# Moving x statistics, Gram products, expert choices and row sends to other places of a hand-written order

## The chip, the cores and the metric

One NeuronCore of a Trainium2 chip runs the whole program. The metric is the device time of one execution in microseconds. The matmul engine is TensorE (PE in the rows, PEld its weight loads), the others are VectorE (DVE), ScalarE (ACT), GpSimd (POOL) and SyncE (SP, which only issues DMAs here).

## What is computed

Two layers over x of shape 4 x 2048 x 256, in float32: an attention over channels, then a mixture of experts.

```python
x = x + layernorm(attn(layernorm(x)))          # attn: per head, softmax over DH x DH products qk . qk
h = layernorm(x) * g + b
logits = h @ Wr;  top 2 of 7 experts, gates = softmax of the two logits
pos = running count of tokens per expert       # a token above the capacity is dropped
routed = sum over choices of gate * (silu(h_e @ W1) * (h_e @ W3)) @ W2
shared = silu(h @ W1s) * (h @ W3s) @ W2s
x = x + layernorm(routed + shared)
```

## The kernel before

A **chunk** is 512 rows; a batch has four of them, q = 0 to 3. The attention of a batch needs only the Gram product of its normalised x (256 x 256, over all 2048 rows); from it comes one matrix M per batch, and the attention's output is x times M. So every batch b has these **steps**, each a few instructions on one or more engines:

- x steps, per chunk: `x_first` (SP loads x chunks 0 and 1), `x_stats` (DVE mean and variance, POOL the power -1/2), `x_norm` (DVE normalises into one of two buffers; behind it SP loads the chunk after next), `x_high` and `x_part` (ACT and DVE split the normalised x into two halves for exact products), `x_gram` (PE, 8 matmuls of 512 columns into banks 4 and 5).
- turned x, per chunk: `x_turned` (SP loads the transposed raw x, 512 KB, into the same two buffers `xin` that held x), `x_keep` (ACT copies its high half), `x_low` (DVE the rest).
- M: the steps `m_gram` to `m_low`, small and in a chain across PE, ACT and DVE.
- output, per chunk: `o_mix` (PE, x times M), `o_stats`, `o_norm`, `o_apply`, `o_add`, `u_stats`, `u_norm`, `u_turn0`, `u_turn1`, `u_route`, `u_copy`: second layernorm, transposition, logits.
- routing, per pair of chunks: `r_top` and `r_next` (DVE, the best and second expert), `u_count` (PE, running counts by matmul), `u_slot` (DVE, adds the carry), `u_place` (DVE, the target rows), then `u_send0` to `u_send3` per chunk (POOL, two indirect DMAs each) that write the rows to memory by expert.

Under all this runs the **shared expert** over the first 13 chunks. Each chunk has eight m-steps; PE does the up products of one m (12 matmuls of 512 columns, a product for the silu first and then one for the factor), then the down products of m-3 (12 matmuls of 256 columns). ACT does the silu (L1114), DVE multiplies (L1801), ACT makes the high half (`high`, L1066) and DVE the low half (`low`, L1777), one m behind. Only two banks take the up products of these chunks, so the up products of m wait for the silu and the multiplication of m-1.

All steps hang on **places**: place 16n+2m lies behind the up products of m-step m of chunk n, place 16n+2m+1 behind the down products that follow. An order written by hand, `schedule`, holds for each place the steps that come there, and every engine walks through the same list (`attend`, L546), doing those that it has a part in. So a step's place sets the order on five in-order queues at once. Within a place, steps of the earlier batch come first. On ACT place 2m comes after the silu of m and place 2m+1 after `high` of m-1; on DVE place 2m comes after the multiplication of m and 2m+1 after `low` of m-1 (and, for m = 6, after the split of the next chunk's h, L1771). ACT also takes the finished chunk before out of its banks (`take_y`) at m = 2, after `high` of m-1.

Waits that matter: `x_gram` waits for `x_part` of its chunk. The load of turned chunk 0 waits for `x_norm` of chunk 2, that of turned chunk 1 for `x_norm` of chunk 3, since they take the buffers that these read:

```python
            def load_turned(b, q):
                ...
                if b > 0 and q > 1:
                    sp.wait_ge(xtlo_ok, b * GB + (q - 1))
                    sp.sem_inc(sp_go, 1)
                sp.wait_ge(xn_ok, OPEN + b * GB + (q % 2 + 3))
                sp.sem_inc(sp_go, 1)
                sp.dma_start(turned_at(b, q).rearrange("p k n -> p (k n)"), x_turned[b * GB + q]).then_inc(xT_in[q], 16)
```

`u_count` waits for `r_next`; `u_turn0` of chunk 3 waits for `u_norm` of that chunk and for `u_slot` of the first pair. After the 13 chunks come the seven routed experts and three held chunks of the shared expert (from about 610 us); their code is the same before and after.

Of the kernel before, what the change touches and what calls it, by code (L numbers as in the profile page):

```python
# [45 lines left out]
def sandwich_kernel(nc, x_in, Wqk, Wv, Wo, tau, ln_g, ln_b, Wr, W1, W3, W2, W1s, W3s, W2s, x_turned, out):  # L46
# [51 lines left out]
    with ExitStack() as ctx:  # L98
# [366 lines left out]
        def put(b, origin, q, names):  # L465
            for name, at in names:
                schedule[BEFORE + origin + at].append((name, b, q))

        X_STEPS = (("x_stats", 0), ("x_norm", 3), ("x_high", 4), ("x_part", 5))
        GRAM_AT = (None, (9, 12, 16, 19), (7, 11, 15, 19), (7, 11, 15, 19))  # L470
        T_STEPS = (("x_turned", (13, 16, 18, 20)), ("x_keep", (16, 18, 22, 25)), ("x_low", (17, 19, 24, 28)))
        M_STEPS = ("m_gram", "m_turn", "m_cross", "m_sym", "m_times_wqk", "m_keep_t", "m_dots", "m_pick", "m_rowdiag",
                   "m_logits", "m_exp", "m_softmax", "m_times_wo", "m_keep_n", "m_times_wv", "m_high", "m_low")
# [11 lines left out]
        def put_routing(b, origin, pairs, firsts, apart):  # L485
            for pair in range(2):
                put(b, origin, pair, zip(R_NAMES, pairs[pair]))
            for q in range(GB):
                put(b, origin, q, [(f"u_send{t}", firsts[q] + apart * t) for t in range(GT)])
# [23 lines left out]

        X_AT, M_AT, MIX_AT = (None, 14, 66, 115), (None, 34, 87, 136), (None, 46, 101, 148)
        for b in range(1, B):
            put(b, X_AT[b] - 8 if b > 1 else 0, 0, [("x_first", 0)])
            for q in range(GB):
                put(b, X_AT[b] + 4 * q, q, X_STEPS)
                put(b, X_AT[b], q, [(name, places[q] - (b == 1 and q == 3 and name == "x_low")) for name, places in T_STEPS])
                put(b, X_AT[b], q, [("x_gram", GRAM_AT[b][q])])  # L520
            put(b, M_AT[b], 0, zip(M_STEPS, M_AT_PLACES[b]))
            for q in range(GB):
                put(b, MIX_AT[b] + 5 * q, q, O_STEPS)
            if b == 1:
                put_routing(b, MIX_AT[b], ((21, 21, 23, 24, 25), (32, 34, 38, 39, 40)), (27, 35, 43, 51), 2)
            elif b == 2:
                put_routing(b, MIX_AT[b], ((21, 21, 22, 23, 24), (31, 32, 33, 34, 35)), (26, 33, 40, 47), 2)
            else:
                put_routing(b, MIX_AT[b], ((21, 21, 24, 25, 26), (31, 31, 34, 34, 35)), (27, 31, 36, 40), 1)
        for j in range(PIECES):  # L530
# [1456 lines left out]
```

## Time and profile before

| | |
|---|---|
| time, median of 3 runs (lowest, highest) | 1077.16 us (1076.68, 1078.14) |
| the profiled execution: its time, its span | 1078.76 us, 1077.0 us |
| granted TensorE clock, mean over the span | 0.995 |
| PE busy, DVE busy | 1046.2 us, 658.9 us |

The span is counted from the first to the last instruction; the profile gives every instruction its start, and for each idle time the engine that ended it. The places 0 to 207 lie between 54 us and 610 us, so a place is 2.7 us on average. PE's rows tell at which place it is: 12 products with `sb_h`, then an even place, 12 with `sb_act`, then an odd one. `L1210` rows are the Gram products, `L1345` rows the start of a count.

### The profile page before, as it was taken

To read this page: it belongs to the slowest core of one execution; us is meant where nothing else is said; L and a number is where in the kernel's file an instruction comes from. 1 tells how busy PE (TensorE), PEld (TensorE's weight loads), DVE (VectorE), ACT (ScalarE), POOL (GpSimd) and SP (SyncE) were. 2 spreads that over 40 slices of the span, in tenths; PEclk is the share of its full clock that TensorE was granted. 3 is DMA by queue.
4 is the path that set the end of the run, shared out by engine and by line. 5 is a ranking of instruction groups with operands and counts; after the bars stand their busy time and mean duration, and the time that the engine had idled before them with its cause. 6 is when DMAs were issued, how large, how long until landed. Compare 5 with 4: busy or idle time off the path is not lost.

```text
span 1077.0 us, 19528 instructions
## 1 busy us (share of the span) xinstructions
PE 1046.2 (97%) x6863; PEld 956.7 (89%) x6863; DVE 658.9 (61%) x1717; ACT 504.3 (47%) x895; POOL 385.4 (36%) x348
## 2 busy tenths in 40 slices
PE   7999999999999989999999999999999999999997
PEld 6888888887889877888888999999999999998886
DVE  7768863787655797537755345455454546364785
ACT  4344452443443444434444345545464636354773
POOL 3011441513531116421167313344443333123563
PEclk9999999999999999999999999999999999999999
DMA  8332351434522135423244145243433423256695
GB/s 285 110 101 83 125 186 40 142 118 142 183 74 89 60 138 165 159 81 136 108 141 162 38 168 145 53 125 71 110 91 86 118 55 86 45 159 228 113 205 114
DMA packets 47949, 130.20 MB, mean 121 GB/s; under 512 B 10356, under 2 KB 18168, under 8 KB 47872
## 3 DMA queue, kind: packets, MB, share of 16 engines
q1 hardware_dynamic: 29376, 93.87, 25.7%
q0 software_dynamic: 18496, 35.35, 14.5%
q8 instruction: 43, 0.70, 0.3%
q14 instruction: 34, 0.28, 0.1%
HBM read 74.24 MB, written 54.93 MB: 120 GB/s over the span
## 4 chain that ended last, share of the span: by engine, by line
PE 88%; DVE 8%; issue 2%; ACT 1%; DMA 1%; DVEq 0%; SPq 0%; POOL 0%; ACTq 0%
PE bank L1191 27%; PE bank L1193 26%; PE bank L1192 26%; PE bank L1210 3%; DVE sb_act L1801 1%; PE bank L1317 1%; PE bank L1370 1%; ACT sb_ln_o L999 1%; PE bank L1270 1%; DVE sb_st L1494 1%; PE bank L1329 1%; DVE sb_act_lo L1777 1%; DMA sb_ysb<-in_L_ffn_W2s_dram 1%; PE bank L1240 1%; DVE sb_stX L1494 0%
## 5 line engine op out<-in xcount | busy, mean ns | idle before, releaser
L1801 DVE TENSOR_TENSOR sb_act<-bank,sb_act 128x512 f32<-128x512 f32 (+2 forms) x240 | 148.6, 619 | 344.0 <-PE bank L1193 319.6
L1191 PE MATMUL bank<-sb_h_hi,sb_wup_lo 128*128 128x512 f32 (+2 forms) x960 | 354.3, 369 | 2.3 <-ACT sb_act L1114 1.5
L1193 PE MATMUL bank<-sb_h_hi,sb_wup_hi 128*128 128x512 f32 (+2 forms) x960 | 349.8, 364 | 0.0
L1192 PE MATMUL bank<-sb_h_lo,sb_wup_hi 128*128 128x512 f32 (+2 forms) x960 | 349.5, 364 | 0.0
L1114 ACT ACTIVATE sb_act<-bank 128x512 f32<-128x512 f32 (+2 forms) x240 | 129.9, 541 | 356.2 <-PE bank L1193 346.0
L1191 PE MATMUL bank<-sb_wdn_hi,sb_act_lo 128*128 128x256 f32 (+1 forms) x848 | 244.8, 289 | 0.6 <-DVE sb_act_lo L1777 0.6
L1193 PE MATMUL bank<-sb_wdn_hi,sb_act_hi 128*128 128x256 f32 (+1 forms) x848 | 238.9, 282 | 0.0
L1192 PE MATMUL bank<-sb_wdn_lo,sb_act_hi 128*128 128x256 f32 (+1 forms) x848 | 238.8, 282 | 0.0
L1191 PEld LDWEIGHTS bank<-sb_h_hi,sb_wup_lo 128*128 128x128 f32 x960 | 180.7, 188 | 23.2 <-DVE sb_act L1801 2.1
L1193 PEld LDWEIGHTS bank<-sb_h_hi,sb_wup_hi 128*128 128x128 f32 x960 | 180.6, 188 | 22.6
L1192 PEld LDWEIGHTS bank<-sb_h_lo,sb_wup_hi 128*128 128x128 f32 x960 | 181.1, 189 | 17.0
L1777 DVE TENSOR_TENSOR sb_act_lo<-sb_act,sb_act_hi 128x512 fp32r<-128x512 f32 (+2 forms) x240 | 147.4, 614 | 27.3 <-ACT sb_act_hi L1066 25.7
L1191 PEld LDWEIGHTS bank<-sb_wdn_hi,sb_act_lo 128*128 128x128 f32 (+1 forms) x848 | 158.3, 187 | 5.7 <-issue 1.2
L1192 PEld LDWEIGHTS bank<-sb_wdn_lo,sb_act_hi 128*128 128x128 f32 (+1 forms) x848 | 158.3, 187 | 3.4
L1193 PEld LDWEIGHTS bank<-sb_wdn_hi,sb_act_hi 128*128 128x128 f32 (+1 forms) x848 | 158.2, 187 | 0.0
L1066 ACT ACTIVATE sb_act_hi<-sb_act 128x512 fp32r<-128x512 f32 (+2 forms) x240 | 136.6, 569 | 1.1 <-DVE sb_act L1801 1.1
L892 POOL DMA_INDIRECT y_scratch<-sb_ysb,sb_scur x42 | 77.3, 1840 | 155.2 <-ACT sb_ysb L1103 90.4
L804 POOL TENSOR_TENSOR sb_rstdB<-sb_veB,sb_mhalf 128x4 f32<-128x4 f32 x16 | 19.1, 1193 | 174.1 <-DVE sb_veB L1620 174.1
L820 POOL DMA_INDIRECT sent_scratch<-sb_rows,sb_sendto x64 | 68.5, 1070 | 30.5 <-issue 18.8
L853 POOL DMA_INDIRECT sb_rows<-sent_scratch,sb_gcur x42 | 43.7, 1041 | 76.9 <-issue 52.2
L999 ACT ACTIVATE sb_ln_o<-bank,sb_nbiasB,sb_rstdB 128x256 f32<-128x256 f32 x64 | 30.9, 563 | 34.9 <-DVE sb_nbiasB L1625 34.9
L800 POOL TENSOR_TENSOR sb_rstdX<-sb_veX,sb_mhalf 128x4 f32<-128x4 f32 x16 | 20.1, 1254 | 72.7 <-DVE sb_veX L1512 72.7
(268 smaller groups left out, 1239.4 us busy)
## 6 DMA issues: line engine op xcount, KB each, us to landing
sb_xin<-in_L_ffn_W_dram SPq DMA_DIRECT2D x28, 512.0 KB, 3.6
sb_x<-in_L_attn_x_dram SPq DMA_DIRECT2D x16, 512.0 KB, 4.2
out_dram<-sb_x SPq DMA_DIRECT2D x16, 512.0 KB, 3.5
sb_xin<-in_L_attn_x_dram SPq DMA_DIRECT2D x14, 512.0 KB, 4.6
sb_xin<-in_x_turned_dram SPq DMA_DIRECT2D x14, 512.0 KB, 4.5
sb_xn<-in_L_ffn_W_dram SPq DMA_DIRECT2D x14, 512.0 KB
hT_scratch<-sb_hr SPq DMA_DIRECT2D x13, 512.0 KB, 2.9
sb_hfull<-hT_scratch SPq DMA_DIRECT2D x13, 512.0 KB, 4.2
```

Of the source, the lines that this page charges most:

```text
L820: pool.indirect_dma_start(sent_d, bass.IndirectOffsetOnAxis(ap=sendto[:, q, t, c:c + 1], axis=0), u[q][:, t, :], None).then_inc(sent[q], 16)
L853: pool.indirect_dma_start(rows[0:w, part, t, :], None, sent_d, bass.IndirectOffsetOnAxis(ap=gcur[0:w, part, t:t + 1], axis=0)).then_inc(ga ...
L892: pool.indirect_dma_start(y_d, bass.IndirectOffsetOnAxis(ap=scur[0:w, par, part, t:t + 1], axis=0), ysb[0:w, part, t, :], None, compute_op ...
L999: ins = s.activation(ln_o[:, t, :], bank[o_bank(b, q) + t // 2][:, (t % 2) * D:(t % 2 + 1) * D], ACT.Identity, scale=rstdB[:, t:t + 1], bi ...
L1066: s.activation(act_hi[:, m % 4, 0:c.w], act[:, m % 3, 0:c.w], ACT.Copy).then_inc(ahi_ok, 1)
L1114: s.activation(act[:, m % 3, 0:c.w], a[:, 0:c.w], ACT.Silu).then_inc(silu_ok, 1)
L1191: t_.matmul(o, a_lo, b_hi, start=start, stop=False, skip_group_check=True)
L1192: t_.matmul(o, a_hi, b_lo, start=False, stop=False, skip_group_check=True)
L1193: return t_.matmul(o, a_hi, b_hi, start=False, stop=stop, skip_group_check=True)
L1210: ins = t_.matmul(bank[4 + k][:, o:c], a[:, k * P:(k + 1) * P], a[:, o:c], start=(q == 0 and t == 0), stop=(q == GB - 1 and t == GT - 1))
L1777: v.tensor_tensor(act_lo[:, m % 4, 0:c.w], act[:, m % 3, 0:c.w], act_hi[:, m % 4, 0:c.w].bitcast(F32), ALU.subtract).then_inc(alo_ok, 1)
L1801: v.tensor_tensor(act[:, m % 3, 0:c.w], bank[(4 if c.wide and m % 2 else 0) + 1][:, 0:c.w], act[:, m % 3, 0:c.w], ALU.mult).then_inc(act_o ...
```

## The change

No instruction is added or taken away. For batches 2 and 3 the x steps get a table of their own, `X_PLACES`, in place of one pattern; the table of batch 1 gives its old places. The turned-x steps, the M steps and the output steps stay where they are. In the routing of batches 1 and 2 some places move.

| step | before (chunks 0, 1, 2, 3) | after |
|---|---|---|
| batch 2: `x_first` | 58 | 56 |
| `x_stats` | 66, 70, 74, 78 | 64, 72, 76, 80 |
| `x_norm` | 69, 73, 77, 81 | 69, 75, 79, 83 |
| `x_high` | 70, 74, 78, 82 | 70, 76, 80, 84 |
| `x_part` | 71, 75, 79, 83 | 71, 77, 81, 85 |
| `x_gram` | 73, 77, 81, 85 | 75, 79, 83, 86 |
| batch 3: `x_first` | 107 | 101 |
| `x_stats` | 115, 119, 123, 127 | 109, 114, 124, 128 |
| `x_norm` | 118, 122, 126, 130 | 115, 124, 128, 132 |
| `x_high` | 119, 123, 127, 131 | 116, 125, 129, 133 |
| `x_part` | 120, 124, 128, 132 | 117, 126, 130, 134 |
| `x_gram` | 122, 126, 130, 134 | 122, 128, 132, 135 |
| not moved: `x_turned`, `x_keep`, `x_low` of chunks 0, 1 | batch 2: 79, 82; 82, 84; 83, 85. Batch 3: 128, 131; 131, 133; 132, 134 | the same |
| batch 1 routing, pairs 0 and 1: `r_next`, `u_count`, `u_slot`, `u_place` | 67, 69, 70, 71; 80, 84, 85, 86 | 67, 69, 70, 74; 78, 82, 83, 89 |
| batch 1, first send of each chunk | 73, 81, 89, 97 | 76, 83, 91, 98 |
| batch 2 routing | 122, 123, 124, 125; 133, 134, 135, 136 | 122, 124, 125, 127; 132, 135, 136, 140 |
| batch 2, first send of each chunk | 127, 134, 141, 148 | 129, 136, 143, 150 |

```diff
@@ -466,8 +466,11 @@
             for name, at in names:
                 schedule[BEFORE + origin + at].append((name, b, q))
 
-        X_STEPS = (("x_stats", 0), ("x_norm", 3), ("x_high", 4), ("x_part", 5))
-        GRAM_AT = (None, (9, 12, 16, 19), (7, 11, 15, 19), (7, 11, 15, 19))
+        X_NAMES = ("x_stats", "x_norm", "x_high", "x_part", "x_gram")
+        X_PLACES = (None, ((14, 17, 18, 19, 23), (18, 21, 22, 23, 26), (22, 25, 26, 27, 30), (26, 29, 30, 31, 33)),
+                    ((64, 69, 70, 71, 75), (72, 75, 76, 77, 79), (76, 79, 80, 81, 83), (80, 83, 84, 85, 86)),
+                    ((109, 115, 116, 117, 122), (114, 124, 125, 126, 128), (124, 128, 129, 130, 132),
+                     (128, 132, 133, 134, 135)))
         T_STEPS = (("x_turned", (13, 16, 18, 20)), ("x_keep", (16, 18, 22, 25)), ("x_low", (17, 19, 24, 28)))
         M_STEPS = ("m_gram", "m_turn", "m_cross", "m_sym", "m_times_wqk", "m_keep_t", "m_dots", "m_pick", "m_rowdiag",
                    "m_logits", "m_exp", "m_softmax", "m_times_wo", "m_keep_n", "m_times_wv", "m_high", "m_low")
@@ -513,18 +516,17 @@
 
         X_AT, M_AT, MIX_AT = (None, 14, 66, 115), (None, 34, 87, 136), (None, 46, 101, 148)
         for b in range(1, B):
-            put(b, X_AT[b] - 8 if b > 1 else 0, 0, [("x_first", 0)])
+            put(b, (0, 0, 56, 101)[b], 0, [("x_first", 0)])
             for q in range(GB):
-                put(b, X_AT[b] + 4 * q, q, X_STEPS)
+                put(b, 0, q, zip(X_NAMES, X_PLACES[b][q]))
                 put(b, X_AT[b], q, [(name, places[q] - (b == 1 and q == 3 and name == "x_low")) for name, places in T_STEPS])
-                put(b, X_AT[b], q, [("x_gram", GRAM_AT[b][q])])
             put(b, M_AT[b], 0, zip(M_STEPS, M_AT_PLACES[b]))
             for q in range(GB):
                 put(b, MIX_AT[b] + 5 * q, q, O_STEPS)
             if b == 1:
-                put_routing(b, MIX_AT[b], ((21, 21, 23, 24, 25), (32, 34, 38, 39, 40)), (27, 35, 43, 51), 2)
+                put_routing(b, MIX_AT[b], ((21, 21, 23, 24, 28), (32, 32, 36, 37, 43)), (30, 37, 45, 52), 2)
             elif b == 2:
-                put_routing(b, MIX_AT[b], ((21, 21, 22, 23, 24), (31, 32, 33, 34, 35)), (26, 33, 40, 47), 2)
+                put_routing(b, MIX_AT[b], ((21, 21, 23, 24, 26), (31, 31, 34, 35, 39)), (28, 35, 42, 49), 2)
             else:
                 put_routing(b, MIX_AT[b], ((21, 21, 24, 25, 26), (31, 31, 34, 34, 35)), (27, 31, 36, 40), 1)
         for j in range(PIECES):
```

## Rows read from the trace of the kernel before

**Rows 1.** The page, part 1: busy us (share of span) x instructions.

```profile
PE 1046.2 (97%) x6863; PEld 956.7 (89%) x6863; DVE 658.9 (61%) x1717; ACT 504.3 (47%) x895; POOL 385.4 (36%) x348
```

**Rows 2.** Timeline of PE, places 69 to 87: start, length, [idle before <-releaser].

```profile
236.12 0.37 PE L1345 MATMUL bank<-sb_oh,sb_earlier 128*128 128x112 bf16 x4 [1.42 <-DVE sb_oh L1701]
...
249.23 2.61 PE L1210 MATMUL bank<-sb_wdn_hi 128*128 128x512 f32 x8 [2.24 <-DVE sb_wdn_hi L1631]
...
257.39 0.50 PE L1191 MATMUL bank<-sb_h_hi,sb_wup_lo 128*128 128x512 f32 x1
...
260.29 0.28 PE L1191 MATMUL bank<-sb_wdn_hi,sb_act_lo 128*128 128x256 f32 x1
...
261.72 1.80 PE L1210 MATMUL bank<-sb_wdn_lo 128*128 128x512 f32 x8
...
263.36 0.39 PE L1191 MATMUL bank<-sb_h_hi,sb_wup_lo 128*128 128x512 f32 x1
...
283.10 1.79 PE L1210 MATMUL bank<-sb_wdn_lo 128*128 128x512 f32 x8
```

**Rows 3.** Timeline of PE, places 121 to 135.

```profile
384.99 0.50 PE L1191 MATMUL bank<-sb_h_hi,sb_wup_lo 128*128 128x512 f32 x1 [1.46 <-ACT sb_act L1114]
...
393.36 0.37 PE L1345 MATMUL bank<-sb_oh,sb_earlier 128*128 128x112 bf16 x4 [1.39 <-DVE sb_oh L1701]
...
426.72 0.37 PE L1345 MATMUL bank<-sb_oh,sb_earlier 128*128 128x112 bf16 x4 [2.01 <-DVE sb_oh L1701]
...
427.26 3.01 PE L1210 MATMUL bank<-sb_wdn_lo 128*128 128x512 f32 x8
```

**Rows 4.** Windows after two of the waits: busy of each engine, PEclk, DMA share, GB/s.

```profile
249.20:256.00 6.80, 6.77 (x26) 5.77 (x27) 2.98 (x7) 1.89 (x3) 1.84 (x2) 0.75 0.50 164
426.70:433.50 6.80, 6.78 (x42) 6.19 (x43) 2.80 (x7) 0.00 (x0) 4.29 (x4) 0.75 0.72 236
```

**Rows 5.** Timeline of DVE: what it idled for at places 64, 109 and 114.

```profile
226.81 0.69 DVE L1777 TENSOR_TENSOR sb_act_lo<-sb_act,sb_act_hi 128x512 fp32r<-128x512 f32 x1 [2.52 <-ACT sb_act_hi L1066]
...
353.67 0.69 DVE L1801 TENSOR_TENSOR sb_act<-bank,sb_act 128x512 f32<-128x512 f32 x1 [2.48 <-ACT sb_act L1114]
...
367.84 0.69 DVE L1777 TENSOR_TENSOR sb_act_lo<-sb_act,sb_act_hi 128x512 fp32r<-128x512 f32 x1 [2.52 <-ACT sb_act_hi L1066]
```

**Rows 6.** Timeline of DVE: one of each kind of work, and what follows it.

```profile
230.71 1.40 DVE L1494 BATCH_NORM_STATS2 sb_stX<-sb_xin 128x6 f32<-128x256 f32 x4
...
232.75 0.69 DVE L1777 TENSOR_TENSOR sb_act_lo<-sb_act,sb_act_hi 128x512 fp32r<-128x512 f32 x1
233.36 0.20 DVE L1697 TENSOR_REDUCE sb_best<-sb_lg 128x8 f32<-128x56 f32 x1
...
247.95 1.22 DVE L1631 TENSOR_TENSOR sb_wdn_hi<-sb_xn,sb_wdn_hi 128x1024 fp32r<-128x1024 f32 x1
...
274.64 1.38 DVE L1523 TENSOR_SCALAR sb_ln_o<-sb_xin,sb_mvX,sb_rstdX 128x256 f32<-128x256 f32 x4
...
435.59 0.27 DVE L1731 SCALAR_TENSOR_TENSOR sb_lost<-sb_place_of,sb_lostid 128x112 f32<-128x112 f32 x1
...
437.51 0.69 DVE L1777 TENSOR_TENSOR sb_act_lo<-sb_act,sb_act_hi 128x512 fp32r<-128x512 f32 x1 [0.21 <-DVE sb_sendto L1743]
...
450.86 0.69 DVE L1801 TENSOR_TENSOR sb_act<-bank,sb_act 128x512 f32<-128x512 f32 x1 [1.22 <-PE bank L1193]
```

**Rows 7.** DMA issues from 264, 275, 411 and 416 us: count, KB, us to landing.

```profile
sb_xin<-in_x_turned_dram SPq DMA_DIRECT2D x1, 512.0 KB, 3.8
...
sb_xin<-in_x_turned_dram SPq DMA_DIRECT2D x1, 512.0 KB, 4.2
...
sb_xin<-in_x_turned_dram SPq DMA_DIRECT2D x1, 512.0 KB, 5.4
...
sb_xin<-in_x_turned_dram SPq DMA_DIRECT2D x1, 512.0 KB, 4.6
```

**Rows 8.** Timeline of ACT, batch 1: its copy of the second turned x chunk.

```profile
131.60 1.06 ACT L971 ACTIVATE sb_wup_hi<-sb_xin 128x1024 fp32r<-128x1024 f32 x1 [0.33 <-DMA sb_xin<-in_x_turned_dram]
```

## The prediction

> **What bounds the kernel now.** I read the page first: PE is busy 97% of the span [rows 1]. The work is the same before and after, so a moved step changes the time only where PE waits, or where its clock falls. Then I read the list of whom PE waited for, and looked for each wait in PE's timeline, counting products to know the place. In the stretch that the change touches (places 56 to 156, 195 to 490 us) the larger ones are these. At place 69 the first count of batch 1 waits 1.42 us for `r_next`. At 73 the first Gram product of batch 2 waits 2.24 us for `x_part` [rows 2]. At 122 the up products wait 1.46 us for a silu, at 123 the first count of batch 2 waits 1.39 us, at 134 the second 2.01 us [rows 3]. After the 2.24 and the 2.01 the granted clock is 0.75 in the mean of 6.8 us, which is a quarter of 6.8: 1.7 us lost each time [rows 4]. After 1.42, 1.46 and 1.39 it stays full. I take it that a wait of 2 us or more costs 1.7 on top here. In all of these DVE is late: it carries x statistics, normalisation and choices close together.
>
> **Units.** One m-step of PE is 2.8 to 2.9 us of up products (257.39 to 260.29) and 1.43 of down products (to 261.72); a Gram product is 1.64 (to 263.36) [rows 2]. A count takes 0.54 (426.72 to 427.26) [rows 3]. On DVE, from start to next start: `x_stats` 2.04 (230.71 to 232.75), `low` or a multiplication 0.61, `r_top` with `r_next` 2.76 (233.36 to 236.12, where the count starts), a split of 1024 columns (`x_part`, `x_low`, h) 1.14, `x_norm` 1.30, `u_place` 1.92 (435.59 to 437.51) [rows 6, 2]; `u_slot` 0.6 and `u_copy` 0.2 from their number of small operations. On ACT a copy of 1024 columns occupies 0.95 to 1.06 [rows 8], silu and `high` 0.55. A turned chunk lands 3.8 to 5.4 us after its issue [rows 7].
>
> **Stretch A, places 64 to 87 (batch 2).** `x_stats` of chunk 0 goes from 66 to 64. There DVE idles 2.52 us, since ACT is in `o_apply` [rows 5]; the 2.04 fit in, if the load is there, and `x_first` is issued earlier too. So `r_next` ends 2.04 earlier and the wait of 1.42 goes; with the restart 1.5. `u_place` (1.92) leaves place 71 and chunk 1's statistics (2.04) leave place 70, both ahead of `x_part`, and the Gram product is asked for one m-step later: the 2.24 and the 1.7 go. The up products that start at 257.39 then start at about 251.9 (257.39 less 1.5, 2.24 and 1.7; the Gram product is ahead of them either way).
>
> But the normalisations of chunks 2 and 3 move from 77 and 81 to 79 and 83, and the turned loads and `x_keep` stay. Followed from 251.9: DVE multiplies at 255.1 (up products plus 0.3), then has, to the end of chunk 2's `x_norm` at 79, two multiplications and two `low`, `u_copy`, one `x_stats`, two splits, the choices and `x_norm`: 11.0, so 266.1. SP issues the turned load 0: landed 3.9 later, 270.0. `x_keep` and `high` on ACT, 271.5. DVE: `low`, `u_slot`, `x_low`, `x_norm` of chunk 3, 3.65, to 275.1. Turned load 1 issued 275.3, landed with 4.2 at 279.5. **ACT stands in `x_keep` of chunk 1 at place 84 until then**; behind it in its queue are `x_high` of chunk 3, `high` and `take_y`, and behind these the next silu. `x_keep`, `x_high`, `high`: 282.0. DVE: `low`, `x_low`, `x_part`: 284.9. PE comes to the Gram product of chunk 3 (place 86) after: two m-steps 260.4, a wait of 0.5 for `x_part` of chunk 1 and the product 262.5, one m-step 266.7, up, count, down, Gram 273.1, one m-step 277.4, up 280.2. It waits 4.7 and then loses 1.7. That product began at 283.10 before, ahead of up products (2.8) that are now done: 284.9 - 283.10 - 2.8 + 1.7 = **+0.7**. Both removed waits are given back. With the two loads at 3.8 each it is +0.2, with 5.4 each +3.5.
>
> Batch 1 shows the distance: there chunk 3 is normalised at 29 and turned chunk 1 is copied at 32, and ACT still waits 0.33 us for the load [rows 8]. Batches 2 and 3 had three places too, and now have one.
>
> **Stretch B, places 109 to 135 (batch 3).** The statistics of chunks 0 and 1 go to 109 and 114, where DVE idles 2.48 and 2.52 us [rows 5]: free. Without them `o_norm` at 119 comes over 1 us earlier, and without `x_high` at 119 the silu at 122 is in time; the choices of batch 2 lose an `x_norm` ahead of them and the count gets a place more. So 1.46, 1.39 and the smaller wait at 128 (0.46, with slower products around) go, about 4.4 with restarts. New: `u_slot` now stands at 125 on DVE, behind a split of h and `u_norm`, and `u_turn0` at 127 needs it: 1.3 by the same adding up. So PE is 3.1 early at 134: it comes to the up products of m = 3 at 418.7 (before: 426.72 less the wait 2.01, less 2.9, 421.8), and to those of m = 2 at 412.8. DVE multiplies at 415.9, then choices, `x_low`, `x_norm` of chunk 3 (all at 132): 5.8, 421.7. The load lands 0.15 + 4.6 later, 426.5. ACT waits for it from 419.5 at place 133; `x_keep`, `x_high`, silu: 428.9. DVE: multiplication, `x_low`, `x_part`: 431.9. PE is at the Gram product of chunk 3 at 423.5: a wait of 8.4 and the clock. It began at 427.26, ahead of down products (1.43) that are now done, and had the clock loss too: 431.9 - 427.26 - 1.43 = **+3.2**. With 3.8 for the load +2.4, with 5.4 +4.0.
>
> **The rest.** `u_place` of batch 1 at 89 stands before `m_sym`, which PE needs at 90; DVE has time from its old place 86 freed, so I take 0.1 (bounds 0 and 1.92). `u_slot` of batch 2 at 136: 0.2. `u_place` of batch 2 at 140 is ahead of `m_pick`, after which DVE idled 1.22 [rows 6]: 1.92 - 1.22 = 0.7. Together **+1.0**, bounds 0.2 and 2.8. The sends take POOL some 20 us for two chunks and are 0 to 4 places later; the next power that DVE needs from POOL stands at 102 and 149, over 10 us after they end: 0, and if that cover went, at most the 2.5 us of one `u_send`. `x_first` earlier on SP waits for nothing: its buffers are free by 42 and 94.
>
> **Sum.** 0.7 + 3.2 + 1.0 = +4.9 on the profiled execution's 1078.76: 1083.7. That one is 1.6 above the median, so the median becomes 1082.1; I say 1082.0. What follows place 156 is unchanged and PE is its bound, so it all comes later by as much. Its own range: low ends 0.2, 2.4, 0.2 give 1080.0, high ends 3.5, 4.0, 2.8 give 1087.5.
>
> A sentence of the Trainium skill speaks for less: its page "DMA: Bandwidth & Descriptors", section "Anatomy of one DMA — SWDGE (gpsimd) path", puts a transfer at about 2.0 us fixed plus its bytes over 436 GB/s. For 512 KB that would be 3.2 us, an estimate for another path than SyncE's, and with it for all three loads the sum would be about 3 lower, 1079. The trace does not agree: 3.8 is the shortest of the four [rows 7].
>
> **Rivals.** *The turned loads hold nobody* (faster): ACT finds them landed, and all removed waits stay removed: A gives 5.4 less 0.5, B 4.4 - 1.3 + 2.0 + 1.7, the rest costs 1.0: -10.7, 1066.5. For it speaks that before the change no load held PE; against it that the two new waits of PE are reckoned at 4.7 and 8.4. It decides where the chains are over 7 us shorter in sum, so that less than -2.2 is left: three loads of under 2.2 us, or DVE some 3 us further ahead at each last `x_norm`. *One stretch only* (about no change): A's wait stays under 2 us and keeps its clock, B's comes: -4 + 3.2 + 1.0, 1077. Speaks for it that A's wait hangs on two loads and DVE's order. *Longer* (slower still): the loads take the 5.4 us of the longest row or more, and another wait passes 2 us and costs the clock: the high ends of A and B and the rest, 1087.5. It has for it that sends and h loads share the DMA engines there. The change doing nothing is excluded by the waits themselves.
>
> **Chances.** Forecast 0.64, longer 0.11, about no change 0.11, faster 0.14. 0.2% is 2.2 us, about what a measurement can tell. So slower 0.75, same 0.11, faster 0.14. The range of 8 in 10 reaches from 1075.0, leaving out the faster rival, to 1087.0.
>
> **What would show it.** The profile after should have: no PE wait at the first counts and at Gram product 0 of batch 2; ACT idle for `in_x_turned` for some 4 us near 279 and 7 near 426; PE waiting for `x_part` at the last Gram product of batches 2 and 3, 4 to 5 and 8 us, each with half clock behind it; DVE without idle before `o_norm`'s followers at 109 and 114. Wrong it would be if ACT does not wait at `x_keep` of chunk 1, or the last Gram products start with no wait.

## The result, and the profile after

The changed kernel takes 1084.78 us (median of four runs, 1084.18 to 1085.41); the kernel before, run beside it, 1077.62 (four runs, 1076.68 to 1078.14). The ratio is 1.0067, with a 95% interval of 1.005 to 1.0085: slower, by 7.2 us. The profiled execution after took 1084.18 us with a span of 1082.4, against 1078.76 and 1077.0: +5.4. Mean granted clock of its span: 0.992 (before 0.995). In the experiments below one run of `x2_only` and one of the kernel before took 2075.5 and 2075.4 us, against 1067 to 1085 in all others; nothing here explains them, and they move the medians given by at most 0.1 us.

The work is the same. The page of the kernel after, part 1 (to be held against [rows 1]):

```profile
PE 1047.1 (97%) x6863; PEld 957.5 (88%) x6863; DVE 659.0 (61%) x1717; ACT 505.3 (47%) x895; POOL 392.8 (36%) x348
```

Lines after L470 have numbers two higher than before: L1212 is the Gram product, L1193 the up and down products, L1347 the count. Whom PE waited for from 200 to 600 us, after the change (total us, times, longest):

```profile
PE bank L1212 <- DVE sb_wdn_lo L1633: 13.2, 3, 8.1
PE bank L1257 <- DVE sb_hr L1575: 1.2, 2, 0.6
PE bank L1193 <- ACT sb_ln_o L1001: 1.1, 1, 1.1
PE bank L1319 <- DVEq L1728: 0.8, 1, 0.8
PE bank L1263 <- DVE sb_hr L1603: 0.4, 1, 0.4
```

The waits for the choices (1.42, 1.39, 2.01) and for the silu (1.46) of [rows 2, 3] are gone, and the Gram product's 2.24 too. In their place stands one line of 13.2 us: a Gram product waits for the low half that `x_part` makes (`sb_wdn_lo`). PE's timeline shows where:

```profile
234.08 0.38 PE L1347 MATMUL bank<-sb_oh,sb_earlier 128*128 128x112 bf16 x4
...
249.67 1.91 PE L1212 MATMUL bank<-sb_wdn_hi 128*128 128x512 f32 x8
...
284.71 0.80 PE L1212 MATMUL bank<-sb_wdn_lo 128*128 128x512 f32 x1 [4.71 <-DVE sb_wdn_lo L1633]
...
401.44 0.63 PE L1319 MATMUL bank<-sb_ident,sb_early 128*128 128x128 f32 x4 [0.78 <-DVEq L1728]
...
431.94 3.35 PE L1212 MATMUL bank<-sb_wdn_lo 128*128 128x512 f32 x8 [8.06 <-DVE sb_wdn_lo L1633]
...
456.00 0.41 PE L1257 MATMUL bank<-sb_hr,sb_headmask 128*128 128x32 f32 x2 [0.59 <-DVE sb_hr L1575]
```

The first two rows have no bracket where [rows 2] had 1.42 and 2.24: the early waits are gone. The row of 284.71 is the first of that Gram product's eight matmuls. The third and fifth are the Gram product of chunk 3, in batch 2 and in batch 3.

Why `x_part` is late is in the chain of work that ended last, followed back from 290 us (start, length, what):

```profile
273.61 1.39 DVE sb_ln_o L1525 x4
275.08 4.03 DMA sb_xin<-in_x_turned_dram
279.62 0.48 issue
280.10 1.04 ACT sb_wdn_lo L967
281.14 0.53 ACT sb_act_hi L1068
281.73 0.57 issue
282.30 0.88 DVE sb_wup_lo L1535
283.19 0.25 issue
283.44 1.23 DVE sb_wdn_lo L1633
284.71 3.29 PE bank L1212 x8
```

Read downward: DVE normalises chunk 3 and so frees the buffer; only then does SP's load of the second turned chunk start; when it has landed, ACT makes its copy and the high halves that had queued up behind it; DVE makes the low halves, that of the turned chunk (L1535) ahead of the one that PE needs (L1633); PE starts. In batch 3 the same chain runs from 420.82 to 431.94, with 4.18 us of load. Before the change no such transfer was on that path: `x_high` of chunk 3 stood two places ahead of that copy in ACT's queue (82 and 84, 131 and 133); now both have the same place, and the copy comes first. ACT's own timeline shows it standing in the copy (L973, `x_keep`), in batch 2 and in batch 3:

```profile
279.14 1.06 ACT L973 ACTIVATE sb_wup_hi<-sb_xin 128x1024 fp32r<-128x1024 f32 x1 [4.12 <-DMA sb_xin<-in_x_turned_dram]
280.10 1.04 ACT L967 ACTIVATE sb_wdn_lo<-sb_ln_o 128x1024 fp32r<-128x1024 f32 x1
281.05 0.61 ACT L1068 ACTIVATE sb_act_hi<-sb_act 128x512 fp32r<-128x512 f32 x1
...
426.41 1.06 ACT L973 ACTIVATE sb_wup_hi<-sb_xin 128x1024 fp32r<-128x1024 f32 x1 [6.13 <-DMA sb_xin<-in_x_turned_dram]
```

DVE, which does `x_part`, was not what came late: in the rows below it has idled 5.11 us at 281.69 for ACT's `high` (in batch 3 it is 6.22 us at 428.93, for ACT's silu). The three idle times of [rows 5] are filled as meant, for the same instructions now wait under half a microsecond (DVE after):

```profile
226.34 0.69 DVE L1779 TENSOR_TENSOR sb_act_lo<-sb_act,sb_act_hi 128x512 fp32r<-128x512 f32 x1 [0.48 <-ACT sb_act_hi L1068]
...
281.69 0.69 DVE L1779 TENSOR_TENSOR sb_act_lo<-sb_act,sb_act_hi 128x512 fp32r<-128x512 f32 x1 [5.11 <-ACT sb_act_hi L1068]
...
354.25 0.69 DVE L1803 TENSOR_TENSOR sb_act<-bank,sb_act 128x512 f32<-128x512 f32 x1 [0.44 <-ACT sb_act L1116]
...
368.43 0.69 DVE L1779 TENSOR_TENSOR sb_act_lo<-sb_act,sb_act_hi 128x512 fp32r<-128x512 f32 x1 [0.48 <-ACT sb_act_hi L1068]
```

And the clock, in the windows behind the two new waits (columns as in [rows 4], which had 0.75 twice):

```profile
284.70:291.50 6.80, 6.79 (x30) 6.01 (x31) 1.15 (x2) 1.62 (x4) 0.00 (x0) 0.77 0.84 323
431.90:438.70 6.80, 6.75 (x18) 5.64 (x19) 0.59 (x1) 0.81 (x2) 1.43 (x1) 0.55 0.92 337
```

0.77 is 0.23 x 6.8 = 1.6 us lost, 0.55 is 3.1 us (the lower of the two levels, 1.2 GHz, until 438.0 by finer windows): in batch 3 the up products of 435.10 and 435.52 still start 0.42 us apart, where those of 438.27 and 438.50, at full clock, have 0.23 between them.

### The profile page after: what moved, and what is told of

It is laid out like the page before. It is cut to its first block, busy times and chain, and to the rows that moved or that the text cites. A ratio compares the mean times of both kernels' runs of the same rounds, so it can differ in the third digit from the quotient of the medians.

```text
span 1082.4 us, 19528 instructions
## 1 busy us (share of the span) xinstructions
PE 1047.1 (97%) x6863; PEld 957.5 (88%) x6863; DVE 659.0 (61%) x1717; ACT 505.3 (47%) x895; POOL 392.8 (36%) x348
## 3 DMA queue, kind: packets, MB, share of 16 engines
q0 software_dynamic: 18496, 35.35, 14.6%
## 4 chain that ended last, share of the span: by engine, by line
PE 88%; DVE 6%; issue 2%; DMA 2%; ACT 1%; DVEq 0%; SPq 0%; POOL 0%; ACTq 0%
PE bank L1193 27%; PE bank L1195 27%; PE bank L1194 26%; PE bank L1212 3%; PE bank L1319 1%; DVE sb_act L1803 1%; PE bank L1372 1%; DMA sb_xin<-in_x_turned_dram 1%; PE bank L1331 1%; PE bank L1272 1%; PE bank L1242 1%; DMA sb_ysb<-in_L_ffn_W2s_dram 1%; DVE sb_h_lo L1773 1%; DVE sb_ln_o L1525 0%; DVE sb_wdn_lo L1633 0%
## 5 line engine op out<-in xcount | busy, mean ns | idle before, releaser
L1193 PE MATMUL bank<-sb_h_hi,sb_wup_lo 128*128 128x512 f32 (+2 forms) x960 | 354.1, 369 | 0.4 <-DVE sb_act L1803 0.4
L1193 PE MATMUL bank<-sb_wdn_hi,sb_act_lo 128*128 128x256 f32 (+1 forms) x848 | 244.6, 288 | 0.6 <-DVE sb_act_lo L1779 0.6
L1193 PEld LDWEIGHTS bank<-sb_h_hi,sb_wup_lo 128*128 128x128 f32 x960 | 180.8, 188 | 20.3 <-issue 1.4
L1193 PEld LDWEIGHTS bank<-sb_wdn_hi,sb_act_lo 128*128 128x128 f32 (+1 forms) x848 | 158.1, 186 | 5.9 <-issue 1.4
L822 POOL DMA_INDIRECT sent_scratch<-sb_rows,sb_sendto x64 | 71.0, 1110 | 51.5 <-DVEq L1748 32.7
```

The source lines that it names most:

```text
L822: pool.indirect_dma_start(sent_d, bass.IndirectOffsetOnAxis(ap=sendto[:, q, t, c:c + 1], axis=0), u[q][:, t, :], None).then_inc(sent[q], 16)
L1193: t_.matmul(o, a_lo, b_hi, start=start, stop=False, skip_group_check=True)
```

## The experiments

**The theory.** ACT stands in `x_keep` of turned chunk 1 until its load lands, because the load may start only after `x_norm` of chunk 3, and the copy is one place behind that. All queued behind it on ACT, `x_high` of chunk 3 above all, is late, and PE with it. **Rival one:** DVE is simply too full near the last chunk, and `x_part` would be late with or without the copy. **Rival two:** the moved choices, target rows and sends (the routing) cost the time. Each diff below is against the changed kernel. The kernel before ran beside all of them, 1078.07 us in the first set (`x2_only`, `x3_only`, `routing_only`, `keep_late`), 1077.68 in the second. The ratios are those of the record and differ a little from quotients of the medians. A difference between kernels of different sets is good to some 0.5 us, by how far the medians of the kernel before lie apart (1077.62, 1078.07, 1077.68).

| kernel | us, median | ratio to before (95%) | against the changed kernel | PE waits at Gram product 3, batch 2 / 3 |
|---|---|---|---|---|
| changed | 1084.78 | 1.0067 (1.005 to 1.0085) | | 4.71 / 8.06 |
| `x2_only` | 1080.78 | 1.0028 (1.0018 to 1.0038) | -4.0 | 5.41 / none |
| `x3_only` | 1081.03 | 1.0028 (1.0017 to 1.0038) | -3.8 | none / 5.63 |
| `routing_only` | 1077.13 | 0.999 (0.998 to 1.0) | -7.7 | none / 1.67 |
| `keep_late` | 1070.17 | 0.9931 (0.9914 to 0.9948) | -14.6 | none / 1.73 |
| `keep2_late` | 1077.28 | 1.0 (0.9991 to 1.001) | -7.5 | none / 8.17 |
| `norm_early` | 1073.36 | 0.9957 (0.994 to 0.9973) | -11.4 | 1.90 / 1.82 |
| `place_back` | 1083.32 | 1.0057 (1.004 to 1.0074) | -1.5 | 5.22 / 8.17 |
| `best` | 1067.50 | 0.9907 (0.989 to 0.9924) | -17.3 | none / 0.75 |

### The parts of the change alone

`x2_only` keeps the new places of batch 2's x steps alone, `x3_only` those of batch 3, `routing_only` the choices, counts, target rows and sends. The edits put the other lines of the change back, for `x2_only`:

```diff
-                     ((109, 115, 116, 117, 122), (114, 124, 125, 126, 128), (124, 128, 129, 130, 132),
-                     (128, 132, 133, 134, 135)))
+                     ((115, 118, 119, 120, 122), (119, 122, 123, 124, 126), (123, 126, 127, 128, 130),
+                     (127, 130, 131, 132, 134)))
-            put(b, (0, 0, 56, 101)[b], 0, [("x_first", 0)])
+            put(b, (0, 0, 56, 107)[b], 0, [("x_first", 0)])
-                put_routing(b, MIX_AT[b], ((21, 21, 23, 24, 28), (32, 32, 36, 37, 43)), (30, 37, 45, 52), 2)
+                put_routing(b, MIX_AT[b], ((21, 21, 23, 24, 25), (32, 34, 38, 39, 40)), (27, 35, 43, 51), 2)
-                put_routing(b, MIX_AT[b], ((21, 21, 23, 24, 26), (31, 31, 34, 35, 39)), (28, 35, 42, 49), 2)
+                put_routing(b, MIX_AT[b], ((21, 21, 22, 23, 24), (31, 32, 33, 34, 35)), (26, 33, 40, 47), 2)
```

> Only the x steps of batch 2 have their new places; batch 3 and the routing stand as before. My theory (the load of turned chunk 1 holds ScalarE behind the late x_norm of chunk 3): the waits of 1.42 and 2.24 us with its clock loss go, and 4 to 5 us of wait with a clock loss come at the last Gram product of batch 2, so within 1 us of the kernel before. Rival (batch 2's places cost nothing, the loss is all of batch 3): 4 to 6 us faster than before.

> Only the x steps of batch 3 have their new places. My theory: a wait of about 7 us at the last Gram product of batch 3 (r_next is behind x_norm here, so the load is issued 1.3 us earlier than with the whole change) with a long half clock; 2 to 4 us slower than before. Rival (the loss comes from the routing places): faster by 3 us or more.

> Only the choices, counts, target rows and sends have their new places; all x steps stand as before. My theory (these places themselves cost only 0.2 us at m_sym and 0.8 us at m_pick, and take 1.92 us from in front of x_part and give the counts a place more): 4 to 7 us faster than before, with no half clock. Rival (later sends or target rows hold the output steps): slower than before by 1 us or more.

PE's timeline at the last Gram product, first of `x2_only`:

```profile
285.71 3.36 PE L1212 MATMUL bank<-sb_wdn_lo 128*128 128x512 f32 x8 [5.41 <-DVE sb_wdn_lo L1633]
```

and of `x3_only`:

```profile
429.52 3.35 PE L1212 MATMUL bank<-sb_wdn_lo 128*128 128x512 f32 x8 [5.63 <-DVE sb_wdn_lo L1633]
```

Each table alone brings the wait in its own batch and leaves the other batch as it was, and in both ACT has stood for the turned load (4.81 us in `x2_only` at 279.51, 4.52 in `x3_only` at 423.99). `x2_only` was slower by more than I gave it (+2.7 where I had said within 1 us), for its wait is 5.41, 0.7 longer than in the whole change, and the window behind it has a clock of 0.70. Some 0.6 us of that wait is `u_slot` of batch 1's second pair: without the new routing it stands at place 85, and DVE does it (282.76) ahead of `x_low` and `x_part`. `x3_only` is 3.0 slower, as expected, with the wait 1.4 below the 7 I had given it. In its profiled execution batch 3 costs 3.8 us, and 1.8 come back in batch 2, where nothing was changed and the clock happened to stay full (last section).

`routing_only` I had put 4 to 7 us faster; it is 0.9 faster. It does shorten the wait of 2.24 to 0.38, but a new one of 1.77 comes at Gram product 2 of batch 2, since both choices of the second pair now stand at 78 on DVE, ahead of `x_part` of chunk 2 at 79 (before, the second one stood at 80). Two other waits are new, of 1.15 and 0.69 us for a multiplication (399.51, 411.64). So rival two falls: the routing costs nothing by itself. It gains next to nothing by itself, either.

The three differences sum to +2.7 + 3.0 - 0.9 = +4.8, and the whole is +7.2. The parts are not independent: with both batch 3's table and the routing, `r_next` too stands at 132 on DVE, ahead of `x_norm` of chunk 3, whose end starts the load. The wait at 431.94 is 8.06 in the whole and 5.63 in `x3_only`, 2.4 us more. By the two chains 1.4 of it is `r_next`, 0.8 the multiplication ahead of it, which starts later (416.22 against 415.41), and 0.2 the load.

### The copy alone

`keep_late` moves only the copy and its low half for turned chunk 1, three places behind `x_norm` of chunk 3 in both batches, and leaves the change as it is.

```diff
+        LATE = {(2, 1, "x_keep"): 86, (2, 1, "x_low"): 87, (3, 1, "x_keep"): 135, (3, 1, "x_low"): 136}
...
-                put(b, X_AT[b], q, [(name, places[q] - (b == 1 and q == 3 and name == "x_low")) for name, places in T_STEPS])
+                put(b, 0, q, [(name, LATE.get((b, q, name), X_AT[b] + places[q] - (b == 1 and q == 3 and name == "x_low")))
+                              for name, places in T_STEPS])
```

> The whole change, with the copy of turned chunk 1 (x_keep, x_low) later: 86 and 87 in batch 2, 135 and 136 in batch 3, in place of 84, 85 and 133, 134. So x_high and the silu no longer stand behind the load. My theory: both waits at the last Gram products fall to under 2 us, no half clock, 8 to 11 us faster than before, about 1068. Rival (the last Gram products are late for x_norm and DVE's own work, not for ScalarE standing at the load): waits of 4 us or more stay, and it is within 2 us of the changed kernel.

It takes 14.6 us off the changed kernel and is 7.9 faster than the kernel before, just short of the gain expected. The edit does two things, though: it also takes `x_low`, 1.14 us of DVE's work, from in front of `x_part`. That is all the work that DVE is spared, and the waits are shorter by 4.7 and 6.3 us, so rival one falls as the main cause. The whole list of PE's waits of 0.35 us or more between 200 and 490 us, from its timeline (lines are four higher than before here):

```profile
260.28 1.91 PE L1214 MATMUL bank<-sb_wdn_lo 128*128 128x512 f32 x8 [0.41 <-DVE sb_wdn_lo L1635]
...
299.48 0.41 PE L1259 MATMUL bank<-sb_hr,sb_headmask 128*128 128x32 f32 x2 [0.60 <-DVE sb_hr L1577]
...
347.24 0.36 PE L1195 MATMUL bank<-sb_m_hi,sb_wup_lo 128*128 128x256 f32 x1 [1.13 <-ACT sb_ln_o L1003]
...
394.68 0.63 PE L1321 MATMUL bank<-sb_ident,sb_early 128*128 128x128 f32 x4 [0.78 <-DVEq L1730]
...
418.85 1.32 PE L1214 MATMUL bank<-sb_wdn_lo 128*128 128x512 f32 x5 [1.73 <-DVE sb_wdn_lo L1635]
...
441.73 0.41 PE L1259 MATMUL bank<-sb_hr,sb_headmask 128*128 128x32 f32 x2 [0.59 <-DVE sb_hr L1577]
...
448.23 1.13 PE L1265 MATMUL bank<-sb_wvo,sb_hr 128*128 128x256 f32 x4 [0.36 <-DVE sb_hr L1605]
```

The books close. The changed kernel's two waits and their clock are 4.71 + 8.06 + 1.6 + 3.1 = 17.5 us. Here 1.73 is left and a window of clock 0.75 behind it (1.7): 17.5 - 3.4 = 14.1, and 14.6 was measured between the medians, 14.3 between the two profiled executions.

`keep2_late` does it in batch 2 only:

```diff
+        LATE = {(2, 1, "x_keep"): 86, (2, 1, "x_low"): 87}
```

> The whole change, with the copy of turned chunk 1 later in batch 2 only (86, 87). If the two waits are separate and each is PE's own loss: the wait of 4.71 us and its clock loss go, the one of 8.06 us stays; 5 to 6.5 us faster than the changed kernel, 1078 to 1080. If a saved wait in batch 2 is only handed on to batch 3: within 2 us of the changed kernel.

It is 7.5 us faster than the changed kernel, more than I expected, and batch 3 keeps its wait, 8.17. The traces show where it comes from: at the `sb_headmask` products of batch 2 it is 6.65 us ahead (299.35 against 306.00), near the 4.71 + 1.6 = 6.3 of wait and clock; 0.4 more comes in batch 3, where the window behind the wait has 0.62 in place of 0.55. At the same product `keep_late` is 6.5 ahead and 7.8 more behind batch 3. So each batch bears about half.

### The load instead of the copy

If the distance from `x_norm` to `x_keep` is what counts, the other end can be moved too. `norm_early` takes `x_norm` of chunk 3 two places sooner, and its `x_stats` two and one, and leaves the copy:

```diff
-                    ((64, 69, 70, 71, 75), (72, 75, 76, 77, 79), (76, 79, 80, 81, 83), (80, 83, 84, 85, 86)),
+                    ((64, 69, 70, 71, 75), (72, 75, 76, 77, 79), (76, 79, 80, 81, 83), (78, 81, 84, 85, 86)),
...
-                     (128, 132, 133, 134, 135)))
+                     (127, 130, 133, 134, 135)))
```

> The whole change, with statistics and normalisation of chunk 3 earlier (x_stats 78 and 127, x_norm 81 and 130, as far from x_keep as before the change) and x_keep, x_low where they were. If the distance from x_norm of chunk 3 to x_keep of chunk 1 is the cause: ScalarE's idle time for the turned load falls under 2 us in both batches, PE waits 1 to 2 us at the last Gram products, 1069 to 1073. If it is the place of x_keep ahead of x_high that costs, whatever the distance: waits of 4 us and more stay, 1080 or more.

It comes out at 1073.36, 4.3 faster than before and 11.4 faster than the changed kernel, just above what I had expected. Whom ACT waited for in `norm_early` between 200 and 600 us:

```profile
ACT sb_wup_hi L973 <- DMA sb_xin<-in_x_turned_dram: 4.1, 3, 2.0
```

and in the changed kernel:

```profile
ACT sb_wup_hi L973 <- DMA sb_xin<-in_x_turned_dram: 10.2, 2, 6.1
```

Moving either end helps, so it is the distance between the two that lets the load hold ACT. Waits of 1.90 and 1.82 stay at the last Gram products. Of the three waits of ACT here two are for turned chunk 0 (0.88 and 1.96); its copies of turned chunk 1 are these:

```profile
276.76 1.06 ACT L973 ACTIVATE sb_wup_hi<-sb_xin 128x1024 fp32r<-128x1024 f32 x1 [1.30 <-DMA sb_xin<-in_x_turned_dram]
...
417.83 1.07 ACT L973 ACTIVATE sb_wup_hi<-sb_xin 128x1024 fp32r<-128x1024 f32 x1
```

In batch 3 that load holds nobody, and PE waits 1.82 all the same. What `norm_early` leaves as it was is the order: the copy (0.96 us) stands ahead of `x_high` and its low half (1.14) ahead of `x_part`. `keep_late` moves both behind, and is 3.2 us faster than `norm_early`.

### The target rows

`place_back` puts `u_place` of batch 2's second pair back to place 136, ahead of the M steps:

```diff
-                put_routing(b, MIX_AT[b], ((21, 21, 23, 24, 26), (31, 31, 34, 35, 39)), (28, 35, 42, 49), 2)
+                put_routing(b, MIX_AT[b], ((21, 21, 23, 24, 26), (31, 31, 34, 35, 35)), (28, 35, 42, 49), 2)
```

> The whole change, with u_place of batch 2's second pair back at 136 in place of 140. My step: 0.7 to 0.8 us at m_pick and the row-diagonal product go, 0.5 to 1.2 us faster than the changed kernel. Rival (VectorE stands idle for the late last Gram product and u_place at 136 fills that): same sign, not to be told apart by time; by the profile the wait at the row-diagonal product of batch 3 (0.59 us) is gone either way. If it is not gone, the step was wrong.

It is 1.5 us faster than the changed kernel, where I had said 0.5 to 1.2, and the row-diagonal product of batch 3, which waited 0.59 at 456.00, waits no more. The term was real, and the two traces give its size: the transposition of M comes 0.14 us earlier than in the changed kernel, the row-diagonal product 0.89 earlier, so `u_place` is 0.75 between the two. The profiled executions differ by 0.9 in all. Ahead of that, wait and clock at the two last Gram products went +0.9 and -1.0 against each other (clock 0.63 and 0.72, in place of 0.77 and 0.55), though nothing was changed there; one and the same kernel moves by as much between its executions (last section).

### The version that beats both

`best` is `keep_late` with one step more: `x_low` of turned chunk 0 in batch 3 one place later, so that `x_norm` of chunk 3, and with it the load, comes first on DVE.

```diff
+        LATE = {(2, 1, "x_keep"): 86, (2, 1, "x_low"): 87, (3, 1, "x_keep"): 135, (3, 1, "x_low"): 136, (3, 0, "x_low"): 133}
```

> As keep_late, and x_low of batch 3's chunk 0 at 133 in place of 132, behind x_norm of chunk 3 instead of ahead of it. My theory: x_norm of chunk 3, x_high, the silu and x_part each come 1.1 us earlier, the last wait of 1.73 us falls to about 0.6 us and costs no clock; 1067 to 1069. Rival (that wait is ScalarE's take_y or the silu alone): no difference from keep_late, 1070.

1067.50 us (1067.18 to 1067.81): 10.2 faster than before, 17.3 faster than the changed kernel. Its last Gram product of batch 3, and the window behind it:

```profile
418.38 1.90 PE L1214 MATMUL bank<-sb_wdn_lo 128*128 128x512 f32 x8 [0.75 <-DVE sb_wdn_lo L1635]
```

```profile
418.30:425.10 6.80, 6.72 (x37) 5.82 (x38) 2.38 (x6) 3.99 (x6) 5.30 (x5) 1.00 0.47 169
```

The load of turned chunk 1 starts at 414.95 instead of 415.45, the wait goes from 1.73 to 0.75, and the clock stays full. The load itself isn't what PE gains by here, for its copy (418.73) comes behind the start of that product; `x_norm` and with it `x_part` are what comes sooner. One microsecond of wait less gave 2.7 us.

## Why the prediction was right, point by point

**The direction and the mechanism: right.** I had predicted 1082.0 in a range of 1075.0 to 1087.0, slower with 0.75; 1084.78 was measured, inside the range. The steps against the profiled execution after:

| step | predicted | measured after |
|---|---|---|
| count of batch 1 and Gram product 0 of batch 2 | no wait | no wait (234.08, 249.67) |
| turned load 1 of batch 2: issue, landed | 275.3, 279.5 | 275.08, 279.11 |
| PE at Gram product 3 of batch 2, wait | 280.2, 4.7 | 280.00, 4.71 |
| stretch A | +0.7 | +0.3 |
| `u_turn0` at place 127 | 1.3 | 0.78 |
| `x_norm` of chunk 3 done, load landed, batch 3 | 421.7, 426.5 | 422.2, 426.4 |
| PE at Gram product 3 of batch 3, wait | 423.5, 8.4 | 423.88, 8.06 |
| clock behind the two waits | 1.7, 1.7 | 1.6, 3.1 |
| stretch B | +3.2 | +4.0 |
| `u_place` ahead of `m_pick` | 0.7 | 0.8 |
| sum, profiled execution | +4.9 | +5.4 |

The times forecast for batch 3 were reckoned from the start times of the kernel before, without the 0.6 us by which PE is late when batch 3 begins. Less that, 422.2, 426.4 and 423.88 are 421.6, 425.8 and 423.3: each a little early, by 0.7 us at most, above all since the load took 4.2 us where the forecast had 4.6. ACT stood in the copy for 4.12 and 6.13 us, where the forecast had some 4 and 7.

The measured sums come from the same step in both timelines. The down products of place 87 and the transposition of M in batch 3 (place 137) before:

```profile
287.51 0.28 PE L1191 MATMUL bank<-sb_wdn_hi,sb_act_lo 128*128 128x256 f32 x1
...
300.36 0.48 PE L1191 MATMUL bank<-sb_h_hi,sb_wup_lo 128*128 128x512 f32 x1
...
436.14 0.49 PE L1221 MATMUL bank<-sb_ident,sb_ln_o 128*128 128x128 f32 x3
...
450.59 0.30 PE L1255 MATMUL bank<-sb_hr,sb_headmask 128*128 128x32 f32 x2
```

and after:

```profile
287.83 0.28 PE L1193 MATMUL bank<-sb_wdn_hi,sb_act_lo 128*128 128x256 f32 x1
...
300.93 0.48 PE L1193 MATMUL bank<-sb_h_hi,sb_wup_lo 128*128 128x512 f32 x1
...
440.74 0.52 PE L1223 MATMUL bank<-sb_ident,sb_ln_o 128*128 128x128 f32 x3
```

That is +0.32 at place 87 (A), +0.57 at 92 (so `u_place` ahead of `m_sym` cost 0.25, where I had 0.1), +4.60 at 137 (B is 4.60 - 0.57 = 4.03), and with 456.00 above +5.41 at the row-diagonal product. All later work is PE's and moves with it: +5.4 in the span.

**Two terms were off in size.** *The clock of stretch B*: "loses 1.7" was 3.1, since the half clock lasted longer than in [rows 4]. That is more than the whole excess of B (0.8), for PE's wait was 0.3 shorter than forecast and PE 0.2 earlier. With A 0.4 below its forecast, it leaves the 0.5 between +4.9 and +5.4. *The step from the profiled execution to the median*: I took off 1.6 us because the profiled execution of before stood that far above its median, and so came from 1083.7 to 1082.1. The profiled execution after took 1084.18, 0.5 from 1083.7; but it lies 0.6 below its own median. By the medians the change cost 7.2 us, against a forecast of 4.8 (1082.0 less 1077.16). Of the 2.8 us by which the forecast missed 1084.78, 0.5 is the steps, and 2.3 is how the two profiled executions stand to the medians (1.6 and 0.6, and 0.1 of rounding). A difference of single executions is uncertain by such amounts: the kernel before took 1074.9 to 1080.8 in the 39 other runs beside the experiments.

**The assumed rule of 2 us did not hold.** I took a wait of 2 us or more to cost 1.7 of clock. The runs show no such line (last section). For the forecast this was harmless in A and B, where the waits are long, but it would mislead a forecast with waits between 1.7 and 2.2.

**The rivals.** "The turned loads hold nobody" was not what the change does, but it is what `keep_late` and `best` make of it: the price worked out, 1066.5, is near the 1067.50 of `best`. "One stretch only" does not hold: both have their wait. "Longer" holds by a part, for the clock of B, not for the loads: these took 3.9, 4.0, 3.5 and 4.2 us.

The sentence on the Trainium skill ("DMA: Bandwidth & Descriptors", section "Anatomy of one DMA — SWDGE (gpsimd) path") would have had 3.2 us for each of these loads, an estimate, for it speaks of GpSimd's path; the trace does not agree, with 3.5 to 4.2 for these four.

**What stays open.** That loads and copies decide is shown from both ends. The wait that `norm_early` leaves in batch 3 (1.82) is work and order, not the load of turned chunk 1; in batch 2 that load still holds ACT for 1.30 us, and how much of the 1.90 is its share wasn't separated. Nor was the copy moved without its low half.

## What to carry to other kernels

When a step frees a buffer for a load, and another engine copies what the load brings, count the distance between them in time: here one place (2.7 us in the mean) for a load of some 4 us, with work still ahead of the load on the engine that frees the buffer, holds the copying engine, and all that is queued behind it, for 4 to 6 us. With three places it was 0.37 and 2.25 us in `keep_late`, and the step that PE needs stood ahead of the copy there. Both count: the distance, and that what the bottleneck needs is not queued behind the copy. If a step is moved later to make room, move what hangs on the transfer that it releases by as much. And cut waits of one or two microseconds in a PE-bound kernel with care for the last one: the clock behind them can cost as much as the wait.

## What the runs showed of the hardware

The granted clock behind a PE wait was not decided by the wait's length alone. Behind the same wait of 2.24 us at the Gram product of batch 2, the kernel before lost a quarter of its window ([rows 4], 0.75), and `x3_only`, which has the same order there, ran at full clock. The window of `x3_only`:

```profile
249.00:255.80 6.80, 6.79 (x49) 5.74 (x50) 4.54 (x11) 3.01 (x4) 1.83 (x2) 1.00 0.47 163
```

In `norm_early` a wait of 1.90 was followed by 0.75 and one of 1.82 by 1.00:

```profile
282.30:289.10 6.80, 6.76 (x29) 6.02 (x30) 1.18 (x2) 1.44 (x3) 1.91 (x2) 0.75 0.95 349
423.30:430.10 6.80, 6.73 (x37) 5.82 (x38) 2.30 (x7) 2.93 (x5) 4.67 (x5) 1.00 0.97 318
```

Waits of 1.73 (`keep_late`) and 1.77 (`routing_only`) had 0.75 in the window behind them as well, and the one of 0.75 in `best` had 1.00, as had one of 1.67 in `routing_only`. So in these runs a wait of 1.7 to 2.2 us cost either its own length or 1.7 more, and it wasn't settled what decides it. This also spreads the time of one and the same kernel: of the ten runs of `routing_only`, four have a mean clock of 0.999 and 1075.5 to 1076.4 us, six have 0.997 and 1076.9 to 1078.0 us. The kernel before lies at 1074.9 us in its fastest runs (clock 0.998) and at 1080.8 in its slowest (0.993).
